# One block of embedding rows fetched row by row from SyncE instead of by an indirect gather

## What is computed

```python
fm = emb_table[jnp.arange(26)[None, :], cat_idx]          # (512, 26, 128) rows of a table of 26*12500 rows
h = relu(dense_x @ Wd1 + bd1); h = relu(h @ Wd2 + bd2)    # 13 -> 512 -> 256
dense = relu(h @ Wdf + bdf)                               # -> 128
Z = concat([fm, dense[:, None, :]], axis=1)               # (512, 27, 128)
S = einsum('bie,bje->bij', Z, Z)
x = concat([S[:, iu, ju], dense], axis=-1)                # 351 pairs + 128
x = relu(x @ Wt1 + bt1)                                   # -> 1024
x = relu(x @ Wt2 + bt2)                                   # -> 1024
x = relu(x @ Wt3 + bt3)                                   # -> 512
x = relu(x @ Wt4 + bt4)                                   # -> 256
return sigmoid(x @ Wo + bo)
```

## Time and profile before

| | us |
|---|---|
| median of 3 runs | 176.47 (176.35 to 177.85) |
| the profiled execution | 176.1 |
| its span | 174.3 |
| PE busy in the span | 161.2 |
| POOL busy in the span | 99.9 |

### The profile page before, as it was taken

The page is one execution under the profiler, slowest core; times in us unless marked ns, Lnnn a source line. Parts: engine busy times, 40 slices in busy tenths (PEclk is TensorE's granted clock), DMA queues, the critical chain, the costliest instruction groups (busy, mean ns, idle before and its releaser), DMA issues.

```text
span 174.3 us, 3885 instructions
## 1 busy us (share of the span) xinstructions
PE 161.2 (93%) x1691; PEld 115.7 (66%) x1691; DVE 72.2 (41%) x139; ACT 62.4 (36%) x108; POOL 99.9 (57%) x111
## 2 busy tenths in 40 slices
PE   2999999589999998899999999999999999999983
PEld 1334464345768785678787867877877777788971
DVE  5005276786664662553504225163212453411311
ACT  3377597848476772031211121311111230201110
POOL 4777777777777777777777777777775000000000
PEclk9999999999999999999999999999999999999999
DMA  2999999329855422121212121211222000000000
GB/s 60 331 385 264 240 315 342 137 58 310 314 171 175 146 56 52 47 64 45 60 49 58 51 56 54 54 52 50 59 49 60 4 0 0 0 4 0 0 0 0
DMA packets 6674, 18.18 MB, mean 104 GB/s; under 512 B 2309, under 2 KB 2441, under 8 KB 6530
## 3 DMA queue, kind: packets, MB, share of 16 engines
q1 hardware_dynamic: 3330, 11.12, 19.6%
q0 software_dynamic: 3328, 6.82, 14.4%
HBM read 17.93 MB, written 0.00 MB: 103 GB/s over the span
## 4 chain that ended last, share of the span: by engine, by line
PE 59%; POOL 21%; issue 8%; DMA 6%; ACT 2%; DVE 1%; DVEq 0%
PE mp L484 23%; POOL rows L345 21%; PE mp L451 8%; PE mp L507 7%; DMA rows<-in_emb,row_of 5%; PE gp L410 4%; PE gp L400 4%; PE tp L459 4%; PE gp L525 3%; PE tp L548 3%; PE mp L548 1%; DMA idx<-in_cat_idx 1%; ACT zt L634 1%; ACT xth L646 1%; ACT a2h L654 1%
## 5 line engine op out<-in xcount | busy, mean ns | idle before, releaser
L345 POOL DMA_INDIRECT rows<-in_emb,row_of x104 | 99.0, 952 | 33.1 <-issue 28.9
L484 PE MATMUL mp<-w2l,a1h 128*128 128x512 f32 x64 | 26.8, 418 | 0.0
L484 PE MATMUL mp<-w2h,a1h 128*128 128x512 f32 x64 | 26.2, 410 | 0.0
L484 PE MATMUL mp<-w2h,a1l 128*128 128x512 f32 x64 | 25.5, 399 | 0.0
L634 ACT COPY zt<-gp 128x512 f32<-128x512 f32 x16 | 9.4, 586 | 31.4 <-PE gp L400 31.3
L400 PE MATMUL gp<-ident,rows 128*128 128x128 f32 x104 | 16.7, 275 | 3.6 <-DMA rows<-in_emb,row_of 3.5
L400 PEld LDWEIGHTS gp<-ident,rows 128*128 128x128 f32 x104 | 12.7, 140 | 10.0 <-DMA rows<-in_emb,row_of 5.8
L410 PEld LDWEIGHTS gp<-zt 128*32 128x32 f32 x1024 | 11.2, 110 | 8.2 <-issue 6.8
L814 DVE TENSOR_TENSOR raw<-mp,bc 128x512 f32<-128x512 f32 x8 | 5.5, 691 | 25.6 <-PE mp L484 25.6
L410 PE MATMUL gp<-zt 128*32 128x27 f32 x1024 | 13.3, 195 | 1.3 <-DVE zt L785 0.8
L484 PEld LDWEIGHTS mp<-w2h,a1l 128*128 128x128 f32 x64 | 12.1, 189 | 2.9 <-DVE a1l L808 0.9
(11 more groups left out here) (85 smaller groups left out, 246.2 us busy)
## 6 DMA issues: line engine op xcount, KB each, us to landing
w<-in_wt SPq DMA_DIRECT2D x13, 512.0 KB, 5.0
rows<-in_emb,row_of POOLq DMA_INDIRECT x104, 2.8
w<-in_wt SPq DMA_DIRECT2D x3, 468.0 KB
bc<-in_rows SPq DMA_DIRECT2D x1, 1024.0 KB, 6.2
wd_sb<-in_wd SPq DMA_DIRECT2D x1, 512.0 KB, 3.5
w1d<-in_wt SPq DMA_DIRECT2D x1, 512.0 KB, 6.1
bt<-in_rows SPq DMA_DIRECT2D x1, 512.0 KB, 8.6
wdf_sb<-in_wdf SPq DMA_DIRECT2D x1, 128.0 KB, 3.3
```

The source lines that it names most:

```text
L345: pool.indirect_dma_start(out=rows[:, n % RING, :], out_offset=None, in_=emb.rearrange("c v e -> (c v) e"), in_offset=bass.IndirectOffsetO ...
L484: last = pe.matmul(sums_of(t, 2 + h), a[:, k, :], w[:, k, cols], start=(k == 0 and part == 0), stop=(k == M1 - 1 and part == 2))
```

## The change

Block 51 (`BY_HAND`) is no longer gathered by POOL. SP fetches it in 128 transfers of one row of 512 bytes. For each it reads the row's number from `row_of` in SBUF into a register (`value_load`) and issues a DMA whose source address is computed from that register. They go to a buffer of their own, `hand_rows`. They are issued in 13 portions, 8 rows after each of the loads 2 to 10, 12 after loads 11 and 12 together, 12 after `bc`, 16 after load 13 and 16 after load 14. A load n from 2 on now waits for load n - 2 instead of n - 3. PE waits for all 128 transfers ahead of group 7 of the second tile.

```diff
+BY_HAND = 2 * BLOCKS - 1
-IN_FLIGHT = 3
+HAND_ROWS = [8] * (LOADS_12 - 2) + [12] * 2 + [16] * 2
+HAND_FROM = [sum(HAND_ROWS[:n]) for n in range(len(HAND_ROWS))]
+def blocks_gathered(t, g):
+    blocks = [BLOCKS * u + GROUP_FROM[g] + n for u in range(t % 2, t + 1, 2) for n in range(GROUP_BLOCKS[g])]
+    return len([b for b in blocks if b != BY_HAND])
+        hand_rows = sb("hand_rows", [P, E])
+            table = emb.rearrange("c v e -> (c v) e")
+            column = block_column(1, BLOCKS - 1)
+            def rows_by_hand(n):
+                for r in range(HAND_FROM[n], HAND_FROM[n] + HAND_ROWS[n]):
+                    row = sp.value_load(row_of[r:r + 1, column:column + 1], min_val=0, max_val=N_CAT * VOCAB - 1)
+                    sp.dma_start(hand_rows[r:r + 1, :], table[bass.ds(row, 1), :]).then_inc(by_hand, 16)
+            sp.wait_ge(idx_step, 8)
             for n in range(2, LOADS_12):
-                if n >= IN_FLIGHT:
-                    sp.wait_ge(w_in[n - IN_FLIGHT], 16)
+                sp.wait_ge(w_in[n - 2], 16)
                 load_to_split(n)
+                rows_by_hand(n - 2)
             sp.wait_ge(gathered[0][NG - 1], 16 * GROUP_BLOCKS[NG - 1])
             for n in range(LOADS_12, LOADS_12 + 2):
                 load_to_split(n)
+            rows_by_hand(LOADS_12 - 2)
             sp.wait_ge(w_in[LOADS_12], 16)
             sp.dma_start(bc[:], ...)
+            rows_by_hand(LOADS_12 - 1)
             for n in range(LOADS_12 + 2, len(LOADS)):
                 sp.wait_ge(w_in[n - 1], 16)
                 load_to_split(n)
+                rows_by_hand(n - 2)
...
+                    if n == BY_HAND:
+                        continue
...
+                if BLOCKS * t + i0 <= BY_HAND < BLOCKS * t + i0 + nb:
+                    pe.wait_ge(by_hand, 16 * P)
-                pe.wait_ge(gathered[t % 2][g], 16 * nb * (t // 2 + 1))
+                pe.wait_ge(gathered[t % 2][g], 16 * blocks_gathered(t, g))
...
+                    src = hand_rows[:] if block == BY_HAND else rows[:, block % RING, :]
```

More of the change, by code:

```diff
@@ L193, in build @@
         rows_sem = sem("rows_sem")
+        by_hand = sem("by_hand")
         w_mid = sem("w_mid")
@@ L399, in transpose_features @@
                 for n in range(nb):
-                    last = pe.transpose(gp[:, 2 + g % 2, n * P:(n + 1) * P], rows[:, (BLOCKS * t + i0 + n) % RING, :], ident[:])
+                    block = BLOCKS * t + i0 + n
+                    src = hand_rows[:] if block == BY_HAND else rows[:, block % RING, :]
+                    last = pe.transpose(gp[:, 2 + g % 2, n * P:(n + 1) * P], src, ident[:])
                 last.then_inc(ft_ready, 1)
```

## The result

The change makes the kernel much slower: 285.0 us in the median of 4 runs (284.79 to 286.0) against 176.44 us, a ratio of 1.6135 with a 95% interval of 1.6091 to 1.6179. The forecast was 206, with a range of 174 to 240.

What follows compares the result with a forecast made beforehand. PE's work was taken to bound the kernel, until SP's row backlog exceeds its pacing waits. The profiled 176.1 us plus 30.3 us for the late last row made 206.4, given as 206, range 174 to 240.

Steps and rivals of the forecast that it cites:

- What bounds the kernel, and what SP's idle time is worth: PE busy 161.2 of 174.3 us; SP's idle time is pacing, free for rows until its waits are used up.
- What is won: POOL's missing gather removes PE's whole 0.96 us wait before group 7 of the second tile, giving 175.1 us.
- The fit: Rival: SP issues all rows in time, kernel takes 175.1 us; chance 0.24, 0.19 as no change and 0.05 as faster.
- What a row costs SP: SP's time per row, p: issue 0.35, register read 0.20, address arithmetic 0.12, together 0.67 us.
- the forecast's own formula: Kernel time is 176.1 - 55.4 + 128 times SP's time per row, once that is over 0.433 us.
- Bounds from both sides: Lower and upper ends for SP's time per row: 0.33 and some 2.0 us.
- the long read: Rival: SP's register read takes 0.6 us or more; at 1.07 us a row the kernel takes 257.7 us; chance 0.18.
- The backlogs lie on top of one another: Delays of weight loads and rows in SP's queue overlap rather than add; load 14 29.5 us late, last row 30.3.
- That the last rows come last: In SP's queue the last rows set the delay, landing at 100.7 against PE's 70.36: 30.3 us late.
- Where the stalls begin: PE idles 20 to 30 us in pieces between 48 and 101, first before products needing load 10, wanted at 48.30.
- The clock: Effect of PE's idle stretches on its clock, left at 0, with a few us allowed upward.
- The portions fit: Rival: at 0.425 us a row or less SP's loads and rows all come in time, kernel takes 175.1; chance 0.24.

Runs made afterwards that it cites:

- the kernel with four: Against the changed kernel, row numbers copied to memory and back as one line, then read four to an instruction without bounds: 207.75 us.

## Why the prediction was wrong, point by point

- *What bounds the kernel, and what SP's idle time is worth* held. SP's waits absorbed the rows up to a point (0.30 us a row cost nothing), and behind it each further us was a us of the kernel (slope 1.266 at p = 1.27).
- *What is won*, 0.96 us, held in size: 0.6% (1.1 us) measured without rows. That the whole idle time goes did not: 0.43 of 0.96 us stayed. The fit was priced "at -0.8% of the profiled time"; 175.1 against 176.1 is -0.6%, and -0.8% is against the median of 176.47. It changes no chance.
- *What a row costs SP* is the step that failed: p = 0.67 was taken, 1.27 measured. With the forecast's own formula, 176.1 - 55.4 + 128 x 1.27 = 283.3 us, against 284.8 in the profiled kernel. So the path was right and this term of the sum was mis-sized by 0.60 us, 128 times. Term by term: (1) the issue, taken at 0.35, is 0.30. (2) The read of the number, taken at 0.20 after the 203 ns of a small ACT instruction, is 0.50. That row was of another kind: an engine's fixed time with its own operands, not a sequencer's wait for a word from SBUF. (3) Arithmetic, taken at 0.12 with its gaps, has 0.07 of instructions (37 + 29 ns), and some 0.17 with the gaps (0.97 - 0.50 - 0.30), over the 0.12 that stood as its bound from above. (4) The check of the bounds that `min_val` and `max_val` bring was not in the sum at all: 0.30.
- *Bounds from both sides* were drawn (0.33 to some 2.0) and held the value, but the range of the times stopped at p = 0.93, since the long read was given only 0.18. The rival of the long read named the right mechanism with the wrong price for it: 1.07 with a read of 0.60; the read was shorter, and the check made up for it.
- The Trainium skill ("DMA: Bandwidth & Descriptors", section Latency and other measured facts) gives a floor of about 600 ns for one load; the trace has 498 in the median and 434 at the least, so for a word from SBUF it is no floor here. Its other price ("Runtime: NRT & Kernel Launch", section Instruction fetch mechanics), 200 ns per register, is not what a further word from SBUF costs here: 0.03 us. For a single read the 600 ns were nearer, and a sum that went by it would have been 27 us short instead of 79.
- *The backlogs lie on top of one another* held, with one left out, `w4`, which cost 5.0 us only where the rows were out of the way. *That the last rows come last* held at p = 1.27 and not for cheap or few rows. From the issue of load 14 to group 7 PE needed 10.9 to 11.5 us (three runs: 72.14 to 83.02, 155.84 to 166.92, 86.18 to 97.71), so the last rows must take longer than that to count. The forecast gave this path no term of its own. An estimate with its timetable: load 14 goes out at 12.9 + 112 p, and with 11.2 us behind it is late against 70.36 from p = 0.41 on, which is where the line crosses, and not from 0.43.
- *Where the stalls begin* was wrong by the forecast's own p. It looked at load 10 alone. At 0.67 load 6 goes out at 8.25 + 4 x (0.35 + 8 x 0.67) = 31.1, and ACT wanted it landed by then in the kernel before:

```profile
31.13 1.04 ACT L610 CAST w2h<-w 128x1024 fp32r<-128x1024 f32 x1
```

  At p = 1.27 ACT already waits for load 3 (0.83 us, issued at 19.83) and then 8.55 us, until 35.26, for load 4.
- *The clock* was left at 0. It fell, to 0.65 in the mean of the stretch from 40 to 140 us and to 0.50 of full, the lower of its two levels (1.2 GHz), in the stretch from 140 to 180, in which PE was busy for 10 of 40 us, and 0.88 right behind it:

```profile
140.00:180.00 40.00, 9.97 (x90) 7.30 (x90) 4.85 (x8) 5.12 (x9) 7.80 (x9) 0.50 0.12 39
180.00:190.00 10.00, 9.65 (x104) 7.85 (x104) 3.71 (x7) 2.41 (x6) 2.27 (x3) 0.88 0.09 19
```

  (The columns are the stretch, its length, busy us and count of PE, PEld, DVE, ACT and POOL, the granted clock, the DMA share and GB/s.) Ahead of the last wait PE's pace is covered by SP's queue, so the clock accounts for at most the 1.6 us by which the part behind that wait grew, 105.5 against 103.9.
- *The portions fit* was right about the mechanism, since at 0.30 they do, and right to doubt the 0.1 us that it left for the address.

## What to carry to other kernels

A DMA whose address comes from a register costs its issuing engine every instruction ahead of it, not only the issue: here 0.30 us for the DMA and 0.97 for reading, checking and computing one number. Before moving a gather to such a queue, count the instructions of one row, checks included. Then take each thing that stands behind the rows in the queue, the weights as well as the last row, and see when it is wanted; here the tightest of them left 0.41 us a row (53 us for 128). Reading several numbers with one instruction and dropping the check brought the row to 0.52; placed where the queue had 80 us to spare (56 to 136) it was free, but also without use, as no one waited there.

## What the runs showed of the hardware beyond that

- A sequencer's read of one word from SBUF took 498 ns, of four 558, of eight 719.
- A store of one 4-byte word from each of 128 partitions to memory, issued right behind four loads, landed after 12.8 us (5.66 to 18.50) and after 12.5 in the kernel with four. `w1d`, 512 KB and issued 1.5 us before it, landed after 7.2.
- 128 single-row transfers at 0.30 us each beside 512 KB loads and gathers changed nothing that could be measured: 175.84 us with them and 175.61 without.
- A range check on a value read into a register (`min_val`, `max_val`) was a real instruction sequence at run time here: 0.30 us each.
